# Rotary additions of all but each layer's first group on VectorE, and GpSimd's first-part scatters in one row

## The reference

```python
h = rms(x) ; q, k, v = h @ wq, h @ wk, h @ wv      # 16 query heads, 4 key heads, 64 wide
q = q * cos + rot_half(q) * sin                    # rotary position, same for k
k = k * cos + rot_half(k) * sin
x = clip(x + softmax(q k^T / 8 + causal) v @ wo)
h = rms(x) ; probs = softmax(h @ wr)               # 8 experts, the top two of each token
x = clip(x + sum over the 2 experts of weight * (silu(h @ wg[e]) * (h @ wu[e])) @ wd[e])
```

## Time and profile before

| | |
|---|---|
| median of 3 runs | 1905.0 us (1904.42 to 1906.77) |
| the profiled execution's own time | 1908.5 us |
| its span, first to last instruction | 1906.7 us |
| mean granted TensorE clock over the span | 0.994 |
| busy TensorE, VectorE, ScalarE, GpSimd | 96%, 68%, 50%, 29% |
| GpSimd's additions L590 | 128, mean 1142 ns, 146.2 us together |
| VectorE's addition L1612 | 32, mean 640 ns |
| GpSimd's scatters L621 | 128, mean 998 ns |

### The profile page before, as it was taken

One profiled execution on the slowest core, in us unless ns is written; L12 is line 12 of the kernel. 1 busy time (PEld: TensorE's weight loads), 2 busy tenths in 40 slices (PEclk: granted clock), 3 DMA queues, 4 the chain that ended last, 5 costly groups with the idle time before them and its releaser, 6 DMA issues.

```text
span 1906.7 us, 36659 instructions
## 1 busy us (share of the span) xinstructions
PE 1837.7 (96%) x10612; PEld 1358.1 (71%) x10613; DVE 1288.2 (68%) x3173; ACT 948.8 (50%) x3625; POOL 543.9 (29%) x721
## 2 busy tenths in 40 slices
PE   5999999999999999999999999999999999999995
PEld 4888888766667888766667888765667888765663
DVE  3676778764467788764467788864466788865456
ACT  4546776732225777642224777642224777652221
POOL 3752212540032233531032332531022332520014
PEclk9999999999999999999999999999999999999998
DMA  6323220245662330236663331236663431135666
GB/s 159 113 86 110 101 100 2 84 121 146 147 161 80 133 130 6 84 104 147 148 156 94 115 119 39 78 86 149 146 166 78 142 119 44 42 89 148 147 163 172
DMA packets 255292, 212.37 MB, mean 111 GB/s; under 512 B 145826, under 2 KB 226420, under 8 KB 255028
## 3 DMA queue, kind: packets, MB, share of 16 engines
q1 hardware_dynamic: 240808, 174.74, 33.7%
q0 software_dynamic: 13952, 35.33, 6.4%
q10 hardware_dynamic: 380, 0.38, 0.1%
HBM read 137.32 MB, written 73.05 MB: 110 GB/s over the span
## 4 chain that ended last, share of the span: by engine, by line
PE 72%; DVE 10%; ACT 8%; issue 3%; POOL 2%; SPq 2%; DMA 2%; POOLq 0%; DVEq 0%; ACTq 0%
PE ps L927 23%; PE ps L953 12%; ACT parena L1271 8%; PE ps L813 8%; PE ps L893 6%; PE ps L869 3%; PE ps L858 3%; PE ps L843 3%; PE ps L821 3%; PE ps L795 2%; DVE rmax L1618 2%; DVE rope L1598 2%; DVE rope L1602 2%; PE ps L921 2%; POOL qk L590 1%
## 5 line engine op out<-in xcount | busy, mean ns | idle before, releaser
L927 PE MATMUL ps<-arena,xeT 128*128 x1120 | 509.4, 593 | 0.0
L1271 ACT ACTIVATE parena<-ps,nmax 112x112 f32<-112x112 f32 x1024 | 345.5, 388 | 115.9 <-DVE nmax L1619 115.9
L927 PEld LDWEIGHTS ps<-arena,xeT 128*128 128x128 f32 x1120 | 210.3, 190 | 193.2 <-issue 187.0
L590 POOL TENSOR_TENSOR qk<-qk,rope 128x448 f32<-128x448 f32 x128 | 146.2, 1142 | 547.0 <-DVE rope L1602 546.7
L1320 ACT ACTIVATE parena<-ps,er 128x512 f32<-128x512 f32 x140 | 96.2, 687 | 383.5 <-PE ps L927 378.8
L813 PE MATMUL ps<-xnT,wqk_s 128*128 128x224 f32 x1280 | 273.5, 357 | 0.0
L569 POOL DMA_INDIRECT y_in<-sorted_y,pos x114 | 111.2, 976 | 500.1 <-DMA sorted_y<-tarena 396.4
L1271 ACT ACTIVATION_READ_ACCUMULATOR parena<-ps,nmax 112x1 f32 x1024 | 247.0, 241 | 0.0
L893 PE MATMUL ps<-wo_s,oT 128*112 128x256 f32 x1024 | 237.9, 385 | 1.3 <-issue 1.3
L813 PEld LDWEIGHTS ps<-xnT,wqk_s 128*128 128x128 f32 x1280 | 233.5, 191 | 3.1
L1894 DVE SCALAR_TENSOR_TENSOR parena<-parena,ps 128x512 f32<-128x512 f32 x140 | 96.1, 686 | 184.6 <-ACT parena L1320 184.6
(11 more groups left out here) (207 smaller groups left out, 2789.5 us busy)
## 6 DMA issues: line engine op xcount, KB each, us to landing
sorted_y<-tarena SPq DMA_DIRECT2D x140, 128.0 KB
xe<-sorted_x SPq DMA_DIRECT2D x132, 130.0 KB, 2.5
arena<-in_L_ffn_wg_dram SPq DMA_DIRECT2D x32, 512.0 KB, 3.7
arena<-in_L_ffn_wu_dram SPq DMA_DIRECT2D x32, 512.0 KB, 4.6
arena<-in_L_ffn_wd_dram SPq DMA_DIRECT2D x32, 512.0 KB, 5.6
hid_d<-tarena SPq DMA_DIRECT2D x240, 64.0 KB
tarena<-hid_d SPq DMA_DIRECT2D x60, 256.0 KB, 2.8
hid_d<-parena SPq DMA_DIRECT2D x240, 64.0 KB
```

The lines of the kernel that those rows point to most:

```text
L590: pool.tensor_tensor(q, q, rope[m % 2][:, :], ALU.add).then_inc(g_rope, 1)
L927: last = pe.matmul(ps[:, bank, :], xeT[u][:, k, :], w[:, bass.ds(e * 1024 + k * 512, 512)], start=(k == 0), stop=(k == KD - 1))
L1271: last = act.activation(prob[:, n, :], ps[0:S, bank, h * S:h * S + S], ACT.Exp, bias=nmax[:, b % 2, n:n + 1], scale=SCALE, accum_out=rsum[ ...
```

## The change

VectorE adds m = 1 to 4 of the groups 1 to 7 of each layer, at the end of `rotate`, behind a wait for its own product; GpSimd keeps those of group 0. The counts of the semaphores stay as they were. On GpSimd the calls of `add_rotated` leave `attention`, and all 18 scatters of the first part stand at b = 12.

```diff
@@ gpsimd
-            SOONER = (3, 7)
-
             def attention(l):
                 for b in range(B):
...
-                    if g + 1 < NP:
-                        for m in (2, 3, 4) if odd else (1,):
-                            if b == RANK_STEP + 2:
-                                scatter_first(l, 0, SOONER[0])
-                            if b == RANK_STEP + 3 and m == 2:
-                                scatter_first(l, *SOONER)
-                            if b == RANK_STEP + 3 and m > 2:
-                                scatter_row(0, SOONER[1], m - 3)
-                            add_rotated(l, g + 1, m)
+                    if b == RANK_STEP + 2:
+                        scatter_first(l, 0, PARTS[0][1])
                     if b == PARTS[0][1]:
                         out_factors(l, 0)
...
             def move_rows(l):
 
-                scatter_first(l, SOONER[1] + 1, PARTS[0][1])
                 for h in range(1, NPART):
@@ vector, rotate
                     ins = dve.tensor_tensor(out_c, out_c, rope[0][:, :], ALU.add)
                 ins.then_inc(d_rope, 1)
+                if m and g:
+
+                    dve.wait_ge(d_rope, l * 40 + g * LOADS + m + 1)
+                    dve.tensor_tensor(out_c, out_c, rope[m % 2][:, :], ALU.add).then_inc(g_rope, 1)
```

## The result

The kernel after took 1928.45 us (median of 5 runs, 1924.5 to 1933.05), the kernel before 1905.4 (5 runs, 1904.42 to 1906.77). The ratio is 1.0117, with a 95% interval of 1.0104 to 1.0131: **22.3 us slower, 19.8 to 25.0**. 1926 was forecast, between 1914 and 1938. The profiled execution of after took 1925.5 us (span 1923.7).

A forecast was written before the change was run, and what follows sets the result against it. TensorE, busy 96% with no slack in the attention, was taken as the bound. Per layer 3.20 + 0.48 + 1.29 + 0.17 = 5.14 us, 20.6 over four layers, on the median 1905.0 gave 1926, range 1914 to 1938.

The forecast's parts named there:

- 0.64 us at the p = 1 scores: Behind an odd b: TensorE's weight load waits 0.64 us more, as the fourth addition ends at 703.42 instead of 702.79.
- A pair with its boundary: Attention pairs from b = 1 to 10: 0.64 us each, plus 0.08 at each boundary into the next odd b.
- the boundary: Behind an even b: of the 0.65 us addition of m = 1, 0.57 falls into VectorE's idle and 0.08 counts.
- The step: Odd b and boundary: VectorE's excess of 0.4 us over TensorE's delay is covered in even b; cover about 0.3 us.
- The pair b = 11, 12: VectorE leads there, so its whole delay counts: 1.86 us less 0.57, costing 1.29 us a layer.
- The pair b = 13, 14: Scatters between additions: stretched products go, the 0.85 us gain is lost at VectorE's normalisation; costs 0.17 us a layer.
- The 0.57 and 0.88 us of idle before `maxima`: VectorE's idle before `maxima`, 0.57 us in odd b and 0.88 in even b, would be gone.
- rival 3: Scatters hold the VectorE additions beside them, up to a bound of 14 us: 1940; chance 0.03.
- Rival 1: Cover in even b is gone, so a pair costs 1.03 us, not 0.64: 1934; chance 0.14.
- Rival 2: Part of the 0.64 us is no wait: 0.3 a pair, nothing at the boundaries, 1917; chance 0.16.
- Rival 4: Faster: the last addition alone decides, taking 0.62 us instead of 1.14; 15 us saved, 1890; chance 0.04.
- the scatters in one row: 18 scatter DMAs in one row end near 793 instead of 798, costed at nothing either way.

The follow-up runs named there:

- m = 4 alone: Only the addition of m = 4 on VectorE, against the kernel before: ratios 1.0028 (1945.72 us) and 1.0014 (1944.85 us), on two slower chips.
- m = 3 and 4: Additions of m = 3 and 4 on VectorE, scatters as before, against the kernel before: 1944.48 us (ratio 1.0015), again 1943.62 us (1.0004).
- m = 1 alone: Only the addition of m = 1 on VectorE, against the kernel before: 1969.3 us (ratio 1.0141) on a slower chip, 1905.25 us (0.9996) on the faster.
- extra product: The changed kernel plus one unread 128x448 product on VectorE behind the addition of m = 4: 2034.48 us against 1941.24 for the kernel before, ratio 1.0482.
- the run on the faster chip: The changed kernel, unedited, run again against the kernel before on the faster chip: 1928.8 us, ratio 1.0114.
- The same kernel: The kernel before with only the addition of m = 1 moved to VectorE: 1905.25 us on the faster chip, 1969.3 us on a slower one.
- the version with m = 4: VectorE adds m = 4 from group 1 on and m = 1 of group 7, 14 scatters in one row, against the kernel before: 1896.17 us, ratio 0.9946.

## Why the prediction was right

- **The direction and the mechanism.** The additions of m = 2 and 3 stand ahead of the last product on VectorE, and TensorE waits for them. Forecast 0.64 us at the p = 1 scores, found 0.65 (0.88 less 0.23). m = 4 alone, with nothing added ahead of the last product, has no such wait; m = 3 and 4, with 0.65 us ahead of it, wait 0.24.
- **The forecast's sum was 5.14 us a layer, 20.6 in all; the periods of the four layers grew by 20.6.** That the two agree to the tenth is luck: three layers grew by some 0.1 more than forecast, and the first by 0.26 less, since before has a longer period there (29.57 from b = 5) that the forecast did not know of. The parts, layer 1 of after against before:
  - A pair with its boundary, b = 3 to 8: forecast 0.64 + 0.08 = 0.72, found 0.76. By m = 1 alone the boundary is 0.07, so the odd b's additions cost 0.69. This is the term that was mis-sized: `maxima` falls 1.03 us further behind in odd b than with m = 1 alone (15.58 for 14.55, forecast 1.03), and 0.34 of it is made up in the even b (14.41 for 14.75). The step took an excess of 0.4 as covered by "about 0.3"; of 0.39 (1.03 less 0.64) the 0.05 by which the cover falls short comes through. The extra product bears it out: with 0.92 us more the even b still takes 14.41.
  - The pair b = 11, 12: forecast 1.29, plus 0.08 of the boundary; found 1.42. VectorE leads there, as the earlier trace rows showed.
  - The pair b = 13, 14: forecast 0.17, with no boundary behind it in the sum, found 0.13. TensorE's two waits of 0.82 and 1.21 us became one of 2.3, as the step had it: the gain at the scores is lost at the normalisation.
  - b = 1 and 9: 0.70 and 0.71 for 0.72.
- **The 0.57 and 0.88 us of idle before `maxima`** The earlier trace rows went, as forecast: 49.2 us over the kernel became 17.2.
- **Scatters beside additions**: the timeline of after, b = 13 of layer 1:

```profile
798.01 0.94 POOL L612 DMA_INDIRECT sorted_x<-x_sb,pos_x  x1 [0.31 <-issue]
798.03 0.63 DVE L1607 TENSOR_TENSOR qk<-qk,rope 128x448 f32<-128x448 f32 x1
```

  The addition keeps its 0.63 us, so rival 3 falls. The stretched products of b = 13 are gone too; all stand at 0.61 and 0.62. How they had been stretched is in the timeline of before: GpSimd's addition runs from 789.39 to 790.54, and the product that starts beside it at 789.68 ends at 791.03, 0.49 behind it, instead of 0.61 behind its own start. The Trainium skill (SBUF — State Buffer, section "Who interferes with whom") names GpSimd's reads of SBUF as what holds a VectorE operation with two SBUF inputs. The trace agrees: with 16 instead of 128 additions on GpSimd the product's mean is 614 ns for 667. Beside a scatter no product is stretched (0.61 to 0.62 us in after), and beside an addition the shuffle from PSUM is not, either (0.65 to 0.67 in before).
- **Rival 1** (the whole 1.03 counts) would have given periods of 30.3; they are 29.99. It is half a rival: the cover held 0.34 once, and holds nothing more, as the extra product showed. The prediction looked for its end at the second normalisation; it came at the values' weight load (L811). **Rival 2** would have shown less than 0.64 at the scores. **Rival 4** is true for one addition and not for four: its point, less than 0.52 us ahead of the last product, is met by m = 4 alone (nothing ahead, −0.26), and missed by m = 3 and 4 (0.65 ahead, +0.04).
- **What was not forecast:** the clock drops behind b = 13, some 1.6 us each. The sum alone gives 1905.4 + 20.6 = 1926.0; the drops fit the rest of the median of 1928.45. Also, the scatters in one row were said to cost nothing either way: the result and the run on the faster chip show no such cost, while on the two slower chips some 8 us a layer go with the row. The last scatter ended 3.3 us sooner, counted from the start of b = 11 (46.7 for 50.1), where 5 were forecast.

## What to carry to other kernels

When work moves from a helper engine to the engine that feeds the bottleneck, price each piece by what stands behind it before the next meeting, not by its duration on the two engines: the last piece of a run can gain up to the difference in speed (here 0.26 of 0.52 us), every piece ahead of it can cost up to its full length (here 0.30 for m = 3 and 0.65 for m = 2, of 0.65; the 0.65 is a difference of kernels, since m = 2 was not moved alone). So try the split as well as the whole move: on the faster chip, m = 4 of each group with a second small move in group 7 gave −10 us, and all four additions +22; m = 4 alone was timed only on the slower chips, where it gave nothing. And cover is a stock: read how much of it there is (0.34 us) and subtract each excess from it, since an excess of 0.39 is not "covered".

## What was not expected of the hardware

- The same kernel took 1905.25 us on one chip and 1969.3 on another, while the kernel before took 1905.9 and 1941.2. A ratio of two kernels (0.9996 and 1.0141) is not the same on all chips.
- On the slower chips TensorE's semaphore counts can come up to some us behind the modelled ends of its products (3.2 us in the case shown), beside indirect DMAs of GpSimd. The waits before `maxima` that the profile calls "remote" for that add up to 48.0 us in one profile, and the granted clock falls behind them.
- A drop of the granted clock to its lower level for 3.4 us costs the pair in which it falls some 1.6 us, in some executions of a kernel and not in others, though TensorE's wait of 2.3 us ahead of it stands in all that were profiled.
- On the slower chips m = 4 alone gives 28.97 in the first layer and 29.4 to 30.2 in the layers with gathers; the version with m = 4 on the faster chip has 28.97 in all. VectorE is released up to 1.2 us behind the products beside a gather of GpSimd there, 0.03 on the faster chip.
